# A fused recurrent kernel: the fp16 state difference is formed ahead of the transpose, and the full state after it

## What is computed

```python
def cell(h, x):
    gi = x @ W_ih + b_ih
    gh = h @ W_hh + b_hh
    i_r, i_z, i_n = jnp.split(gi, 3, axis=-1)
    h_r, h_z, h_n = jnp.split(gh, 3, axis=-1)
    r = jax.nn.sigmoid(i_r + h_r)
    z = jax.nn.sigmoid(i_z + h_z)
    n = jnp.tanh(i_n + r * h_n)
    h_new = (1.0 - z) * n + z * h
    return (h_new, h_new)
...
return x + hs + spline_delta(layernorm(hs))   # per token: 16 features of the chosen expert's slice
```

## Time and profile before

| what | value |
|---|---|
| time, median of 3 runs | 2601.79 us (2601.41 to 2604.37) |
| the profiled execution | 2604.53 us, span 2602.7 us |
| mean granted TensorE clock | 0.964 |
| busy: PE, DVE, ACT, POOL | 90%, 50%, 26%, 7% of the span |
| input product, 0 to 1011 us | PE busy 991 us |
| HEADS, 1011 to 1249 us | PE 156, DVE 172, ACT 104 us |
| KEPT, 1249 to 1564 us | PE 310, DVE 198, ACT 113 us |
| FULL with LAST, 1564 to 2275 us | PE 701, DVE 466, ACT 252 us |
| DIFFS, 2275 to 2488 us | PE 150, DVE 163, ACT 113 us |
| end, 2488 to 2603 us | PE 47, DVE 67, ACT 7, POOL 56 us |

### The profile page before, as it was taken

The page is one execution under the profiler, slowest core; times in us unless marked ns, Lnnn a source line. Parts: engine busy times, 40 slices in busy tenths (PEclk is TensorE's granted clock), DMA queues, the critical chain, the costliest instruction groups (busy, mean ns, idle before and its releaser), DMA issues. The chain is left out here.

```text
span 2602.7 us, 83556 instructions
## 1 busy us (share of the span) xinstructions
PE 2354.0 (90%) x35300; PEld 1289.6 (50%) x35300; DVE 1291.3 (50%) x2644; ACT 668.9 (26%) x1340; POOL 189.1 (7%) x376
## 2 busy tenths in 40 slices
PE   7999999999999997666999998999999999977734
PEld 3444444444444443333666664666666666633311
DVE  4321121211111133777666664666666666877765
ACT  2200000000000012444333332333333333355520
POOL 0000000000000000000000000011111111121217
PEclk9999999999999998999999998999999999999955
DMA  6543131313131144333344443444444444477722
GB/s 213 182 150 125 53 121 54 121 53 122 51 140 53 49 150 141 95 88 87 120 138 129 136 138 86 122 114 113 114 120 122 113 114 120 122 225 222 221 50 4
DMA packets 160438, 305.21 MB, mean 117 GB/s; under 512 B 26832, under 2 KB 76416, under 8 KB 159296
## 3 DMA queue, kind: packets, MB, share of 16 engines
q1 hardware_dynamic: 122448, 236.06, 28.8%
q10 hardware_dynamic: 27648, 50.34, 5.2%
q0 software_dynamic: 10240, 17.31, 4.5%
HBM read 209.54 MB, written 144.18 MB: 136 GB/s over the span
## 5 line engine op out<-in xcount | busy, mean ns | idle before, releaser
L290 PE MATMUL acc<-w_hi,x_hi 128*128 128x512 f16 x1536 | 584.0, 380 | 19.7 <-DVE x_lo L234 11.2
L291 PE MATMUL acc<-w_hi,x_lo 128*128 128x512 f16 x1536 | 583.9, 380 | 0.0
L292 PE MATMUL acc<-w_lo,x_hi 128*128 128x512 f16 x1536 | 583.7, 380 | 0.0
L483 PE MATMUL rz_bank<-w_hi,hi 128*32 128x512 f16 x6912 | 427.7, 391 | 150.7 <-ACT hi L592 69.5
L242 DVE SCALAR_TENSOR_TENSOR out_stage<-acc,bias_row 128x512 f32<-128x512 f32 x192 | 132.3, 691 | 719.7 <-PE acc L292 719.7
L483 PEld LDWEIGHTS rz_bank<-w_hi,hi 128*32 128x32 f16 x6912 | 177.8, 98 | 326.9 <-ACT hi L592 81.5
L290 PEld LDWEIGHTS acc<-w_hi,x_hi 128*128 128x128 f16 x1536 | 150.6, 98 | 203.0 <-issue 16.0
L483 PE MATMUL rz_bank<-w_lo,hi 128*32 128x512 f16 x4096 | 243.1, 379 | 0.0
L483 PE MATMUL rz_bank<-w_hi,lo 128*32 128x512 f16 x4096 | 243.1, 379 | 0.0
L292 PEld LDWEIGHTS acc<-w_lo,x_hi 128*128 128x128 f16 x1536 | 150.6, 98 | 182.5 <-issue 2.2
L291 PEld LDWEIGHTS acc<-w_hi,x_lo 128*128 128x128 f16 x1536 | 150.6, 98 | 181.7 <-issue 1.7
(11 more groups left out here) (158 smaller groups left out, 2013.8 us busy)
## 6 DMA issues: line engine op xcount, KB each, us to landing
gi<-gi_scratch SPq DMA_DIRECT2D x704, 96.0 KB
gi_scratch<-out_stage ACTq DMA_DIRECT2D x192, 256.0 KB, 2.1
gi<-sums_scratch SPq DMA_DIRECT2D x40, 512.0 KB
xstage<-in_xT SPq DMA_DIRECT2D x32, 512.0 KB, 6.0
y<-in_x_rows SPq DMA_DIRECT2D x32, 512.0 KB, 4.4
hs_scratch<-h SPq DMA_DIRECT2D x128, 128.0 KB
h_tok<-hs_scratch SPq DMA_DIRECT2D x32, 512.0 KB, 3.9
y<-hs_scratch POOLq DMA_DIRECT2D x32, 512.0 KB, 7.8
```

The lines of the kernel that those rows point to most:

```text
L290: nc.tensor.matmul(acc[e % BANKS][:], hi, wh, start=k == 0, stop=False)
L291: nc.tensor.matmul(acc[e % BANKS][:], lo, wh, start=False, stop=False)
L292: last = nc.tensor.matmul(acc[e % BANKS][:], hi, wl, start=False, stop=k == KB - 1)
L483: last = nc.tensor.matmul(bank[q * COLS:(q + 1) * COLS, 0:b - a], state[:, s, j], w[:, j, q * QW + a:q * QW + b], start=first and j == 0, ...
```

## The change

In DIFFS and LAST, VectorE forms `old_less = 256 * z_old - warm_state` right behind `z_old`, and after `new_n` the difference `diff = 256 * new_n + old_less` in fp16, which is transposed straight into `hi`. The full state `h` is formed behind that and is no longer transposed in these modes. `warm_state` must then be untransposed, so `act_keep` copies `h` and not `h_turned`, released by `h_ready`; the wait of KEPT for that copy moves from the transpose to `h`. `old_less` and `diff` lie in `sums`, which has no other use in these modes. Two semaphores per set are new, and `turned` is brought up to its count after the stage. Lines of the changed kernel differ from those before: 702 `rn`, 718 `n_sum`, 720 `z_old`, 724 `old_less`, 728 `new_n`, 733 `diff`, 738 the transpose, 743 `h`, 779 the routing's first line.

```diff
--- before.py
+++ after.py
@@ -369,6 +369,9 @@
     n_act = sb("n_act", [P, SETS, QF])
     z_old = sb("z_old", [P, SETS, QF])
     new_n = n_sum
+
+    old_less = sums[:, :, 0:QF]
+    diff = [sums[:, s, RZ:RZ + QF // 2].bitcast(F16) for s in range(SETS)]
 
     h_start = sb("h_start", [P, SETS, QF])
     next_start = sb("next_start", [P, SETS, QF])
@@ -425,6 +428,7 @@
     saved_hi_ready, saved_lo_ready = set_sems("saved_hi_ready"), set_sems("saved_lo_ready")
     sums_stored, gi_kept, state_out_ready, state_stored, diff_seen = (
         set_sems(n) for n in ("sums_stored", "gi_kept", "state_out_ready", "state_stored", "diff_seen"))
+    old_less_ready, diff_made = set_sems("old_less_ready"), set_sems("diff_made")
     curves_loaded, split_step = sem("curves_loaded"), sem("split_step")
 
     h0_loaded, start_shifted, start_step, gap_step, gap_ready, gap_summed, pass_judged, first_judged = (
@@ -597,9 +601,9 @@
             nc.scalar.activation(saved[:, s, 0], sums[:, s], ACT.Copy, scale=SUM_SCALE).then_inc(saved_hi_ready[s], 1)
 
         def act_keep(act, it, u, s):
-            act.wait_ge(turned[s], steps_to(it, u))
+            act.wait_ge(h_ready[s], steps_to(it, u))
             act.wait_ge(state_stored[s], it * 32 + (u * 16 + 32 - WARM_HEADS * 16))
-            nc.scalar.activation(state_out[:, s], flat(h_turned[:, s]), ACT.Copy, scale=S_SCALE).then_inc(state_out_ready[s], 1)
+            nc.scalar.activation(state_out[:, s], h[:, s, u], ACT.Copy, scale=S_SCALE).then_inc(state_out_ready[s], 1)
 
         def act_diff(act, it, u, s):
             act.wait_ge(hi_ready[s], steps_to(it, u) + 2)
@@ -714,26 +718,34 @@
             nc.vector.tensor_tensor(n_sum[:, s], rn[:, s], gi[:, s, u, QW:RECORD] if mode == DIFFS else gi[:, s, u, RZ:QW], ALU.add)\
               .then_inc(n_sum_ready[s], 1)
             nc.vector.tensor_tensor(z_old[:, s], rz[:, s, QF:RZ], h_old, ALU.mult).then_inc(z_old_ready[s], 1)
+            if mode in (DIFFS, LAST):
+                dve.wait_ge(z_old_ready[s], n)
+                dve.wait_ge(warm_state_loaded[s][u], from_diffs(it) * 8 + 16 * (1 + u))
+                nc.vector.scalar_tensor_tensor(out=old_less[:, s], in0=z_old[:, s], scalar=S_SCALE, in1=warm_state[:, s, u],
+                                               op0=ALU.mult, op1=ALU.subtract).then_inc(old_less_ready[s], 1)
             dve.wait_ge(not_z_ready[s], n)
             dve.wait_ge(n_ready[s], n)
             nc.vector.tensor_tensor(new_n[:, s], not_z[:, s], n_act[:, s], ALU.mult).then_inc(new_n_ready[s], 1)
             dve.wait_ge(z_old_ready[s], n)
             dve.wait_ge(new_n_ready[s], n)
+            if mode in (DIFFS, LAST):
+                dve.wait_ge(old_less_ready[s], from_diffs(it) + (u + 2))
+                nc.vector.scalar_tensor_tensor(out=diff[s], in0=new_n[:, s], scalar=S_SCALE, in1=old_less[:, s],
+                                               op0=ALU.mult, op1=ALU.add).then_inc(diff_made[s], 1)
+                dve.wait_ge(diff_made[s], from_diffs(it) + (u + 2))
+                if mode == DIFFS:
+                    dve.wait_ge(diff_seen[s], from_diffs(it) + (u + 1))
+                nc.vector.transpose(flat(hi[:, s]), diff[s]).then_inc(hi_ready[s], 1)
             if mode not in (HEADS, KEPT):
                 dve.wait_ge(h_stored[s][u], it * 16 + (16 - pair_of(0, 0) * 16))
-            nc.vector.tensor_tensor(h_new, new_n[:, s], z_old[:, s], ALU.add).then_inc(h_ready[s], 1)
-            dve.wait_ge(h_ready[s], n)
             if mode == KEPT:
                 dve.wait_ge(state_out_ready[s], it * 2 + (u + 1 - WARM_HEADS))
+            nc.vector.tensor_tensor(h_new, new_n[:, s], z_old[:, s], ALU.add).then_inc(h_ready[s], 1)
+            if mode in (DIFFS, LAST):
+                return
+            dve.wait_ge(h_ready[s], n)
             nc.vector.transpose(flat(h_turned[:, s]), h_new).then_inc(turned[s], 1)
-            if mode in (DIFFS, LAST):
-                dve.wait_ge(turned[s], n + (seeds - 1))
-                dve.wait_ge(warm_state_loaded[s][u], from_diffs(it) * 8 + 16 * (1 + u))
-                if mode == DIFFS:
-                    dve.wait_ge(diff_seen[s], from_diffs(it) + (u + 1))
-                nc.vector.scalar_tensor_tensor(out=flat(hi[:, s]), in0=flat(h_turned[:, s]), scalar=S_SCALE, in1=warm_state[:, s, u],
-                                               op0=ALU.mult, op1=ALU.subtract).then_inc(hi_ready[s], 1)
-            elif mode != HEADS:
+            if mode != HEADS:
                 dve_low(dve, s, n + seeds)
             if mode == KEPT:
                 dve.wait_ge(saved_hi_ready[s], it * 2 + (u + 1 - WARM_HEADS))
@@ -894,6 +906,7 @@
                         tile(i, (DIFFS, DIFFS), True)
                     for s in range(SETS):
                         dve.sem_inc(lo_ready[s], WARM_FULL + 1)
+                        dve.sem_inc(turned[s], WARM_FULL + 1)
                         dve.sem_inc(rz_sum_ready[s], WARM_FULL)
                         dve.sem_inc(hn_ready[s], WARM_FULL)
                 T = p * TILES + TILES
```

## The result

The changed kernel takes 2597.13 us (median of 14 runs, 2595.71 to 2598.24), the kernel before 2603.24 beside it (14 runs, 2601.21 to 2605.74): ratio 0.9977 [0.9968, 0.9985], 6.1 us less.

What follows compares the result with a forecast made beforehand. A chain through several engines was taken to bound DIFFS, TensorE to cover KEPT. Terms -5.5 + 1.3 + 0.1 + 1.0 + 0.1 = -3.0 us took the median 2601.79 to 2598.8 us; range 2592.5 to 2604.5.

Steps and rivals of the forecast that it cites:

- (a) half-steps: Set a's half-steps in DIFFS, where VectorE then waits for ScalarE: -0.29 and about -0.26 us, -5.5 over ten tiles.
- (b) half-steps: Set b's half-steps in DIFFS, where VectorE works without a pause: +0.07 us each, +1.3 over the first nine tiles.
- The end: After the last set b half-step, the kernel's end is released by `h`, which comes later: +1.0 us.
- KEPT and the others at nothing: In KEPT TensorE's 98% covers the moved waits; in the other stages no instruction changes: 0.
- The fp16 transpose: VectorE's transpose of `diff` into `hi` was taken at 0.45 us, as from fp32, between bounds of 0.25 and 0.45.
- The rival of the copy's pace: VectorE's fp16 transpose runs as fast as a copy, 0.2 us sooner in 42 half-steps: -8.4 us, 2590; chance 0.08.
- Later `h`: Rival: in DIFFS later `h` makes ScalarE's `act_sum` idle about 1.1 us per tile; with late DMAs up to 2616; chance 0.05.
- No overlap: Rival: VectorE's `new_n` and `h` each wait for the instruction before to end: +7.0 us, 2606; chance 0.03.
- A second pass: Rival: changed rounding fails the start-state test, so all 64 steps run again: over 900 us; chance 0.01.
- The operation count: VectorE's operations rise from 7 to 8; by the skill's rule alone every half-step would grow by one spacing.

Runs made afterwards that it cites:

- x1: Kernel before, with ScalarE's square of set a's difference moved behind set b's gates in DIFFS: 2590.48 us, ratio 0.9951.
- x7: x1 with `act_sum` also moved, from behind the tanh of step 0, set b to behind the gates of step 1, set a: 2587.34 us.
- x10: x7 with the copies of `x` into `y` for the last 11 tiles issued in FULL instead of DIFFS: 2576.15 us, ratio 0.9897.
- x8: Changed kernel with KEPT's two waits put back as before, the copied tile still `h`: 2598.62 us, ratio 0.9981.
- x5: Changed kernel with `h` of step 1, set b formed behind `dve_signed` in DIFFS: 2601.78 us, ratio 0.9996.
- x9: Changed kernel with ScalarE's square and token sum later, and copies of `x` into `y` for the last 11 tiles issued in FULL: 2579.16 us.

## Why the prediction was right, and where it was small

It called no change with 0.75. The kernel came out 0.23% faster, and the interval, 0.15% to 0.32%, lies on both sides of the 0.2% bound. The time is within the range; direction and mechanism held; the size was half of the measured one, and the miss of 3.1 us is more than the 2.5 that the prediction gave as its own error. That 2597.13 lies only 1.7 us from the 2598.8 forecast is luck in part: the kernel before, at 2601.79 when the forecast was made, came out at 2603.24 over 14 runs. By its own steps:

- **(a) half-steps.** Forecast -0.29 and -0.26; both measured -0.31. Times 20: -6.2 us for -5.5.
- **(b) half-steps: the term that was mis-sized.** Forecast +0.07 each, measured 0.00. `new_n` came 1.13 behind `n_sum`, not 1.15; the transpose 0.97 behind `new_n`, not 0.99; `h` 0.37 behind the transpose, but the routing only 0.31 behind `h`, which took 0.38 and not 0.42: 0.68 for 0.70. Hundredths, but in 22 half-steps 1.5 us. Each of the spacings had been taken 0.01 to 0.02 above the one measured.
- **The end.** Forecast +1.0; `h` came 2.93 behind `rn` (1.95 before), +0.98, and `act_sum` idled 4.12 for 3.41:

```profile
2488.09 1.06 ACT L615 ACTIVATE xhat<-h_tok 128x1024 f32<-128x1024 f32 x1 [4.12 <-DMA h_tok<-hs_scratch]
```

  The way through DRAM was 0.3 us shorter, and from there on 0.2 less passed than before. The first (0,b) of DIFFS also took 6.09 us before and 5.88 now; its extra 0.2 is one idle time ahead of `csums` in the routing, which x1, x7 and x10 have too and no run of the changed kernel has, and whose cause is open. With these, -6.2 - 0.2 + 0 + 1.0 - 0.5 makes the -5.9 us that the two traces leave for the change. So of the 2.9 us between that and the forecast of -3.0, 1.5 are the (b) half-steps, 0.7 the (a) ones, and 0.7 lies in terms that the prediction did not have.
- **KEPT and the others at nothing.** Shown by x8.
- **The fp16 transpose.** Taken at 0.45; it took 445 ns on the mean of 38, as from fp32. The rival of the copy's pace falls. The Trainium skill, "VectorE: DVE Perf Modes", "The three transpose paths", gives 311 ns for 128x128 in bf16, half our elements; ours took 445 ns for twice as many. Two elements per cycle, which the Trainium skill holds possible in the same page's "What auto-detection actually checks", don't appear here: fp16 took as long as fp32.
- **Later `h`.** Forecast 1.1 us of idle time ahead of `act_sum`, measured 0.45 to 0.81, and nothing followed. The room ahead of `rn` of (1,a), put at 1.3 us, is nearer 1.65 in the changed kernel's trace: `rz` ends at 2388.77, `rn` starts at 2390.52, and elsewhere it starts 0.10 behind `rz`; `act_sum` was done at 2387.57, ahead of `hi` at 2387.65, and took nothing of it. x5 shows that the mechanism exists: with some 2.1 us more delay a tile paid 0.30.
- **No overlap.** Falls: independent neighbours started 0.34 (`new_n`) and 0.36 to 0.37 (`h`) behind the one before.
- **A second pass.** Didn't come.
- **The operation count.** The Trainium skill, "VectorE: DVE Perf Modes", "Rules for kernel authors", says to minimize the number of vector operations. The changed kernel has one more per half-step and is faster, and even its (b) half-steps, for which the prediction let the rule stand, took 5.88 and 5.63 us as before. Where VectorE never pauses (x9, x10) eight against seven came out level, for the eight had fewer long spacings; by the count alone each half-step would have grown by 0.34. The measurement decides: what counts is the spacings on the path, not the number.

## What to carry to other kernels

Where an engine would pause anyway, or in the gap between two dependent instructions, an extra independent one cost 0 to 0.2 us here and not the 0.34 of a place in full work; so split a chain and let what others wait for go first, and price each place by whether its engine pauses right behind it. Look then for who ends the pause: here one square and one sum on ScalarE, moved out of the way, together with the DMAs that this uncovered, were worth four times as much as the change, and took the change's gain with it. A result within a few hundredths per instruction is multiplied by the number of instructions, so add start-to-start distances from the row that has the very same neighbours.

## What the runs showed of the hardware

- A 32x32 block transpose of 128x256 took 445 ns from fp16 as from fp32.
- An instruction behind a transpose started 0.36 to 0.37 us after it and took 0.38 where it takes 0.42 elsewhere; the one behind that started 0.31 later.
- The same product of 32 matmuls took from 1.9 to 3.6 us with the granted clock. In the kernel before:

```profile
2324.50 3.56 PE L483 MATMUL rz_bank<-w_hi,hi 128*32 128x512 f16 x32 [2.40 <-DVE hi L734]
...
2345.66 1.91 PE L483 MATMUL rz_bank<-w_hi,hi 128*32 128x512 f16 x32 [2.40 <-DVE hi L734]
```

  From 2324.5 to 2328.0 us the granted clock was 0.51, about the lower of its two levels of 2.4 and 1.2 GHz, and from 2345.66 to 2347.6 it was 1.00; TensorE had stood 2.40 us for `hi` ahead of either. In x9 a slow product came behind a late load:

```profile
2426.30 1.01 PE L506 MATMUL rz_bank<-gi,ident_sum 128*128 128x512 f16 x2 [3.15 <-DMA gi<-sums_scratch]
...
2427.67 2.88 PE L488 MATMUL rz_bank<-w_hi,hi 128*32 128x512 f16 x32
```

  The granted clock from 2426.0 to 2430.5 us was 0.62. But x9 also has a product of 3.56 us behind a wait of only 0.71 for `hi`, so the load isn't shown to be the cause; what makes the clock fall in one tile and not in the next is open.
- A slow product costs time only where something waits for it. The changed kernel's tiles take 20.54 to 20.57 us, with a granted clock of 1.00 in the five to 2380 us and 0.92 in the four behind them. In x9 the one product above, with the load ahead of it, cost VectorE 1.61 us at an `rn`.
